# Row maxima from the high parts only: two heads as two 64-row tiles of TensorE

## The reference

```
qkv = X @ W_qkv + b_qkv
qkv = qkv.reshape(b, l, H, 3 * DK).transpose(0, 2, 1, 3)
Q, K, V = jnp.split(qkv, 3, axis=-1)
scores = jnp.einsum('bhqd,bhkd->bhqk', Q, K) / np.sqrt(DK)
attn = jax.nn.softmax(scores, axis=-1)
out = jnp.einsum('bhqk,bhkv->bhqv', attn, V)
```

## Time and profile before

| what | value |
|---|---|
| median of 3 runs | 1965.26 us (1964.3 to 1972.4) |
| span of the profiled execution | 1962.0 us (no other time is recorded for that execution) |
| attention | about 75 to 1735 us of the span, 32 pairs of about 52 us |
| PE busy in the whole span | 1813.4 us, 92% |
| DVE busy | 1567.3 us, 80% |
| POOL, ACT busy | 59%, 55% |

### The profile page before, as it was taken

How to read it: one execution, slowest core, us unless ns; L and a number is a source line. 1 busy time by engine, 2 the same in 40 slices (tenths; PEclk the granted TensorE clock), 3 DMA queues, 4 the chain that set the end, 5 groups by cost and what they waited for, 6 DMA issues and landing times. The chain is left out here.

```text
span 1962.0 us, 29122 instructions
## 1 busy us (share of the span) xinstructions
PE 1813.4 (92%) x7819; PEld 985.8 (50%) x7819; DVE 1567.3 (80%) x2879; ACT 1081.5 (55%) x2008; POOL 1166.7 (59%) x521
## 2 busy tenths in 40 slices
PE   4899999999999999999999999999999999956996
PEld 3444444445544445544444444445544444425886
DVE  5788888888788888888787878887788888677788
ACT  4455555555555555555555555555555555424874
POOL 4465666666666666666666666666666666722124
PEclk8899999999999999999999999999999999967999
DMA  2111111111111111111111111111111110100010
GB/s 88 45 37 33 38 35 35 33 37 37 37 37 37 27 37 28 36 37 37 37 37 32 37 32 34 35 37 37 37 37 37 27 37 28 50 22 22 23 38 27
DMA packets 51521, 70.64 MB, mean 36 GB/s; under 512 B 6269, under 2 KB 29338, under 8 KB 51482
## 3 DMA queue, kind: packets, MB, share of 16 engines
q1 hardware_dynamic: 51328, 70.15, 12.9%
q10 hardware_dynamic: 154, 0.03, 0.0%
HBM read 14.58 MB, written 2.10 MB: 8 GB/s over the span
## 5 line engine op out<-in xcount | busy, mean ns | idle before, releaser
L553 POOL TENSOR_TENSOR ACC<-ACC,PR 128x1024 f32<-128x1024 f32 x382 | 924.4, 2420 | 217.8 <-ACT PR L615 211.4
L615 ACT ACTIVATE PR<-ps_s 128x512 f32<-128x512 f32 x1024 | 555.8, 595 | 653.4 <-PE ps_s L819 648.7
L648 DVE TENSOR_REDUCE NMH<-ps_mx 128x1 f32<-128x512 f32 x1016 | 679.1, 677 | 290.4 <-PE ps_mx L805 286.5
L828 PE MATMUL ps_o<-PR,V 128*64 128x512 f32 x2048 | 548.9, 614 | 0.0
L805 PE MATMUL ps_mx<-KA,QA 128*128 128x512 f32 x1016 | 460.1, 454 | 57.4 <-DVE NMH L648 57.1
L805 PEld LDWEIGHTS ps_mx<-KA,QA 128*128 128x128 f32 x1016 | 190.9, 188 | 468.4 <-issue 243.6
L818 PE MATMUL ps_s<-QA,KA 128*128 128x512 f32 x1024 | 406.5, 397 | 0.0
L819 PE MATMUL ps_s<-QB,KB 128*128 128x512 f32 x1024 | 403.7, 394 | 0.0
L553 POOL TENSOR_TENSOR ACC<-PR 128x1024 f32<-128x1024 f32 x64 | 159.7, 2495 | 372.6 <-ACT PR L615 372.6
L683 DVE RECIPROCAL SUM<-SUM 128x128 f32<-128x128 f32 x256 | 241.0, 943 | 6.9 <-ACT SUM L592 5.0
L819 PEld LDWEIGHTS ps_s<-QB,KB 128*128 128x128 f32 x1024 | 192.7, 188 | 46.0
(11 more groups left out here) (188 smaller groups left out, 1627.2 us busy)
## 6 DMA issues: line engine op xcount, KB each, us to landing
hcur<-hT SPq DMA_DIRECT2D x32, 512.0 KB, 2.9
KA<-KA SPq DMA_DIRECT2D x128, 128.0 KB, 2.3
QB<-QA SPq DMA_DIRECT2D x128, 128.0 KB, 2.3
Wraw<-in_L_attn_W_qkv SPq DMA_DIRECT2D x32, 192.0 KB, 2.4
x<-in_L_attn_X SPq DMA_DIRECT2D x4, 512.0 KB, 5.3
Wfc<-in_L_attn_W_fc SPq DMA_DIRECT2D x32, 64.0 KB, 1.8
hT<-in_L_attn_X SPq DMA_DIRECT2D x4, 512.0 KB, 5.8
out<-e_res SPq DMA_DIRECT2D x7, 256.0 KB, 2.3
```

Source lines behind the costliest of these rows:

```text
L553: G.tensor_tensor(ACC[:, ch, :, :], a, PR[:, t, :, :], ALU.add).then_inc(added, 1)
L615: A.activation(PR[:, t, h, :], ps_s[:, h, :], ACT.Exp, scale=SCALE).then_inc(exp_done, 1)
L648: D.tensor_reduce(NMH[:, ch, h, i, kc:kc + 1], banks[:, kc, :], AX, ALU.max, negate=True).then_inc(mx_red, 1)
L828: last = T.matmul(ps_o[half(h), ch, :], V[:, u, t, half(h)], PR[:, t, h, :], start=(t == 0), stop=(t == 7))
```

## The change

`max_half` becomes `max_heads`. A step still does two products for the maxima, each 128 queries by 512 keys, but they are now the two heads for the same 512 keys, not the two halves of the keys for one head. Each uses only the 64 rows of the high parts: head 0 has partitions 0 to 63 of `QA` and `KA`, head 1 has 64 to 127, so that they are two 64-row tiles of the array. The maximum is that of Q high times K high, and so differs a little from the one before; softmax does not depend on it. Both products stand next to each other behind `scores`. They wait together for both reductions of the step before; nothing stands at the end of the step any more. DVE does as many reductions of the same shape, in the same places of its order, and `place` gives the index of query block and key half in place of head and query block.

```
-            def max_half(m, u, ch, h, i, kc, count, banks=ps_mx, ahead=0):
+            def max_heads(m, u, ch, i, kc, count, banks=ps_mx, ahead=0):
...
-                wait(pe, mx_red, 2 * (count - ahead) - 1 + kc)
+                wait(pe, mx_red, 2 * (count - ahead))
                 q = ch * 512 + i * P
-                T.matmul(banks[:, kc, :], QA[:, u, h, q:q + P], KA[:, u, h, kc * 512:(kc + 1) * 512],
-                         start=True, stop=True).then_inc(mx_done, 1)
+                for h in range(2):
+                    T.matmul(banks[:, h, :], QA[half(h), u, h, q:q + P], KA[half(h), u, h, kc * 512:(kc + 1) * 512],
+                             start=True, stop=True).then_inc(mx_done, 1)
...
                 for s in range(16):
-                    d, ch, h, i = place(s)
-                    grp = (n + d, u if d == 0 else 1 - u, ch, h, i)
+                    d, ch, i, kc = place(s)
                     scores(n, u, s)
                     if has(n + d):
-                        max_half(*grp, 0, 16 * n + s + 10)
+                        max_heads(n + d, u if d == 0 else 1 - u, ch, i, kc, 16 * n + s + 10)
                     x = unit_at(n, s)
...
                     if x and x[0] != "rows":
                         v_of_last_step(n, u, s)
-                    if has(n + d):
-                        max_half(*grp, 1, 16 * n + s + 10)
```

More of the change, by code:

```diff
@@ L397, in place @@
             if s < 6:
-                i = s + 2
-                return 0, 1, i // 4, i % 4
+                k = s + 2
+                return 0, 1, k // 2, k % 2
             if s < 14:
[L401 to L404, removed]
+                k = s - 6
+                return 1, 0, k // 2, k % 2
+            k = s - 14
+            return 1, 1, k // 2, k % 2
         UNITS = {0: ("k", 1, 0), 1: ("k", 1, 1), 2: ("sums", -1, 1), 3: ("q", 1, 0),
@@ L640, in split_w, with reduce_max @@
                 last.then_inc(w_lo, 1)
-            def reduce_max(m, ch, h, i, count, banks=ps_mx):
-                if h == 0 and i == 0:
+            def reduce_max(m, ch, i, kc, count, banks=ps_mx):
+                if i == 0 and kc == 0:
                     wait(dve, mx_both, 2 * m + ch - 1)
[L646 to L649, removed]
+                for h in range(2):
+                    dve.wait_ge(mx_done, 2 * count - 1 + h)
+                    D.tensor_reduce(NMH[:, ch, h, i, kc:kc + 1], banks[:, h, :], AX, ALU.max, negate=True).then_inc(mx_red, 1)
+                if i == 3 and kc == 1:
                     dve.wait_ge(mx_red, 2 * count)
@@ L694, in first @@
                 for i in range(8):
-                    reduce_max(0, 0, i // 4, i % 4, i + 1, (ps_mx, ps_s)[i % 2])
+                    reduce_max(0, 0, i // 2, i % 2, i + 1, (ps_mx, ps_s)[i % 2])
                 dve.wait_ge(s_mask, 3)
@@ L699, in first @@
                 for i in range(2):
-                    reduce_max(0, 1, i // 4, i % 4, i + 9)
+                    reduce_max(0, 1, i // 2, i % 2, i + 9)
                 split_w(1, 1)
@@ L704, in pair @@
                 for s in range(16):
-                    d, ch, h, i = place(s)
+                    d, ch, i, kc = place(s)
                     if has(n + d):
-                        reduce_max(n + d, ch, h, i, 16 * n + s + 11)
+                        reduce_max(n + d, ch, i, kc, 16 * n + s + 11)
                     x = unit_at(n, s)
@@ L792, in freed @@
                     pe.wait_ge({"v": v_copied, "rows": neg_rows, "sums": sums_in, "fc": fc_added}[kind], 2 * m + ch + 1)
-            def max_half(m, u, ch, h, i, kc, count, banks=ps_mx, ahead=0):
-                if h == 0 and i == 0 and kc == 0:
+            def max_heads(m, u, ch, i, kc, count, banks=ps_mx, ahead=0):
+                if i == 0 and kc == 0:
                     pe.wait_ge(q_lo, 2 * m + ch + 1)
@@ L836, in first @@
                         for i in range(8):
-                            for kc in range(2):
-                                max_half(0, 0, 0, i // 4, i % 4, kc, i, (ps_mx, ps_s)[i % 2], 1)
+                            max_heads(0, 0, 0, i // 2, i % 2, i, (ps_mx, ps_s)[i % 2], 1)
                         pe.wait_ge(mx_both, 1)
@@ L842, in first @@
                 for i in range(2):
-                    for kc in range(2):
-                        max_half(0, 0, 1, i // 4, i % 4, kc, i + 8)
+                    max_heads(0, 0, 1, i // 2, i % 2, i + 8)
                 freed("q", 0, 1)
```

## The result

| what | before | changed |
|---|---|---|
| median (4 runs each) | 1966.36 us | 2062.27 us |
| ratio, 95% interval | | 1.0486 [1.0468, 1.0505] |
| span of the profiled execution | 1962.0 us | 2061.4 us |
| PE's wait for the reductions, each | 1.49 us | 2.10 us |
| one pair of heads (middle value, 200 to 1600 us) | 52.0 us | 55.2 us |

The changed kernel is 4.9% slower. The direction was forecast and the time lies in the range, but the forecast was 1.8%: of 99.4 us of span only some 35 were in the sum. So most of the question is where the other 64 come from.

What follows compares the result with a forecast made beforehand. PE's list of matmuls plus one wait per pair was taken to bound the kernel: -22.6 + 46.9 + 11 us of waits = +35 on a 1962.0 span, so 1997, and 2001 us as median (1.8% more); range 1910 to 2070.

Steps and rivals of the forecast that it cites:

- Two tiles at once: At the pair of maxima products: two 64-row tiles load and stream together and cost one matmul, 0.235 us.
- (d): Rival: the two tiles stream in turn, so the saved stream is not saved; 2107 us, chance 0.10.
- (c): Rival: the second tile's load waits for the first, +0.105 us in each of 502 steps; 2054 us, chance 0.10.
- A change of the rows costs as much as one of the columns: Around the 64-row pair: each change into a 128-column shape costs 0.19 us, a 0.085 gap plus a 0.105 bare load.
- (a): Rival: a change of the rows costs nothing, so each of 502 steps saves a whole stream; 1878 us, chance 0.12.
- (b): Rival: the 0.085 gap is paid, but 64-row loads run ahead under the matmul; 1930 us, chance 0.12.
- (e): Rival: no change of shape and no concurrency, only 11 us of waits are added; 1976 us, chance 0.08.
- PE's list: PE's matmuls: -0.045 us in each of 502 steps (-22.6), +0.19 in 247 steps with a full-width unit (+46.9).
- The wait at step 5: PE waits for both reductions of step 4, behind the q unit of step 3: a wait of about 0.25 us.
- The wait at step 15: PE's 1.49 us wait behind DVE's chain: data 1.18 earlier, 1.27 more reductions, so it grows by about 0.1 us.
- The clock: PE's granted clock stays at 1.00 (the 2.4 GHz level) throughout, so no time is added for it.

Runs made afterwards that it cites:

- e5: Kernel before, in its order, with each maxima product on only the 64 rows of its head, the two never together: 2192.49 us, ratio 1.1145.
- e15: Kernel before with the join as a one-input reduction and the division's multiplication reading V's sums from PSUM, ACT's copy left out: 1910.63 us.
- e16: Changed kernel with the join as a one-input reduction and the division's multiplication reading V's sums from PSUM, ACT's copy left out: 1944.96 us.
- e1: Kernel before with one more DVE reciprocal of 128 by 128 in step 13, into a buffer nobody reads: 2034.76 us, ratio 1.0342.
- e11: Changed kernel with eight more 128-row products, read by nobody, ahead of the pair in step 15: 2016.42 us, ratio 1.0243.
- e3: Changed kernel's order and waits, but its two products use all 128 rows: 2049.23 us, ratio 1.0422.
- e7: Changed kernel with the full-width or sums unit ahead of the pair of products and the join as a one-input reduction: 1903.5 us, ratio 0.9666.
- e9: Kernel before with the division one step earlier, its last part and multiplication in step 12, none in step 13: 1942.52 us, ratio 0.9885.
- e13: Kernel before with the join as a reduction and the division's last part, with its multiplication, moved from step 13 to 12: 2002.56 us.
- e14: Kernel before with the join as a reduction, the division's second and third parts in step 11 and the last in step 12: 2004.23 us.

## Why the prediction was right and wrong

**Two tiles at once: right.** One row x2 in the profile, 0.43 up to V for one product (e5) as for two. Rivals (d) and (c) fall: there is no second stream and no second load.

**A change of the rows costs as much as one of the columns: right.** 0.32 on the way in and 0.34 from the next full-width matmul to its second, as the earlier trace rows have for columns; +0.39 a step in e5 for two. Rivals (a), (b) and (e) fall with this. The Trainium skill's page "TensorEngine Tiling (Array Packing)" (Key Properties) says that changing the tiling mode drains TensorE; the runs now agree for rows also.

**PE's list: right, a little short.** Predicted were -0.045 and +0.145 a step, with 8 steps of either kind in a full pair +0.80 us, or 46.9 - 22.6 = 24.3 us in all. Between e15 and e16, where the view shows no wait, the steps without a full-width unit are 0.03 shorter in the mean and those with one 0.17 longer, so +1.1 us in a pair: 34 us in 31 pairs, as the two times say.

**The wait at step 5: right in kind, too large.** The view of the waits has one wait in a pair, at step 15. But in step 5 DVE's reductions end at 1026.81, and the pair of products starts at 1026.86, 0.40 behind the last score where other steps have 0.32; the score's modelled end covers that. The step is 0.06 longer than the other plain ones, where 0.25 was forecast.

**The wait at step 15: right in place, mis-sized.** "The wait grows by about 0.1"; it grew by 0.61, 19 us. The step behind it said that the chain's data come 1.18 earlier and that it holds 1.27 more, a reduction at either end; it took the durations on DVE as fixed. They are not: the join's 0.79 was not its own length (0.17 as a reduction that reads the same elements), nor the multiplication's 2.22 (0.69 in e15), but what was left of POOL's sums. So the chain up to the multiplication's end could not move ahead. The 1.18 earlier and the reduction at the front came to nothing, and what stayed is the reduction at the back, 0.64.

**The clock: the step that failed.** "The clock I take as 1.00 throughout, since PE rests nowhere much longer than in the wait of 1.49". It was a sentence about the old wait, and the sum then let that wait grow. Behind 2.10 us the clock falls to 0.59 for four us and costs 1.63 more: 31 × 1.63 = 51 us, the largest term of all. e1 makes it without tiles (43 us), e11 takes it away with the tiles in place (46 us).

The sum by what was measured: 31 × (1.10 + 0.61 + 1.63) = 104 us, against 99.4 in the spans; so the terms are good to some 5 us in all.

What stays open: why steps 3 and 5 of e3 are longer; how long the wait would be if PE waited for one reduction only in the changed order; and whether the e15 edit and e7's order add up, since no kernel had both.

## What to carry to other kernels

A wait of the engine that bounds the kernel is priced with the clock that follows it: read the granted clock in a stretch that begins at the wait's end, and ask what it becomes if the wait grows by half. Count the changes of tile shape, not the streams saved: halving the rows paid here only where the order let two tiles stand together and put them next to something that changes shape anyway (the tiles gave -33 us with the unit ahead of them; the whole change, with the unit behind them, cost +34). And when a short operation takes long, look for what ends at the same time on the neighbouring engine before its duration goes into a chain: an operation that is held does not move ahead when its data do.

## What the runs showed of the hardware

A VectorE operation with two operands in SBUF that begins while GpSimd's sum is under way finishes only behind that sum's end: the join 0.03 behind it, the multiplication 0.55, the split in e9 held up to it. Reciprocals and reductions (one operand), and the multiplication with one operand in PSUM (0.69 in e15), show no such hold in the same places. The Trainium skill's page "SBUF — State Buffer" (SBUF: two separate sides) says that VectorE and GpSimd share a pair of ports as an exclusive lock, which a VectorE operation with two SBUF inputs needs against a GpSimd operation that reads SBUF, for the whole instruction; the rows agree, and looked up for the join and the multiplication it would have warned that their durations in the earlier trace rows's chain are not fixed.

And the clock: behind waits of 1.49 us TensorE keeps the 2.4 GHz level; with 1.80 (e13, e14) the mean of the middle is 0.98; with 2.1 to 2.3 it is 0.97, and 0.59 to 0.68 right behind the wait. One rest of 2.1 us in a pair of some 55 us was enough.
